# Eight-layer gated cross-attention decoder: a new order of the wide attentions' beginnings, side work and one PSUM bank

## The reference

```python
x = x + tanh(g_xattn[0]) * L0_xattn(layernorm(x), ctx, mask)      # stage 0: 8 heads of 64, masked
x = x + tanh(g_ffn[0])   * L0_ffn(layernorm(x))                   # stage 1: 16 gated attention experts
x = x + tanh(g_xattn[1]) * L1_xattn(layernorm(x), ctx)            # stage 2: 8 heads of 64
x = x + tanh(g_ffn[1])   * L1_ffn(layernorm(x))                   # stage 3: spectral
x = x + tanh(g_xattn[2]) * L2_xattn(layernorm(x), ctx)            # stage 4: 16 heads of 8
x = x + tanh(g_ffn[2])   * L2_ffn(layernorm(x))                   # stage 5: 32 experts
x = x + tanh(g_xattn[3]) * L3_xattn(layernorm(x), ctx, mask)      # stage 6: 16 heads of 64, null key, two layernorms
x = x + tanh(g_ffn[3])   * L3_ffn(layernorm(x))                   # stage 7: low rank
```

## Time and profile before

| | us |
|---|---|
| median of 3 runs (lowest, highest) | 3243.49 (3242.99, 3244.15) |
| the profiled execution's own time | 3244.79 |
| its span | 3243.0 |
| TensorE busy in it | 3020.5 (93%) |
| VectorE busy in it | 2210.6 (68%) |
| ScalarE busy in it | 1564.5 (48%) |
| GpSimd busy in it | 1207.0 (37%) |

### The profile page before, as it was taken

The page is one execution under the profiler, slowest core; times in us unless marked ns, Lnnn a source line. Parts: engine busy times, 40 slices in busy tenths (PEclk is TensorE's granted clock), DMA queues, the critical chain, the costliest instruction groups (busy, mean ns, idle before and its releaser), DMA issues. The chain is left out here.

```text
span 3243.0 us, 90979 instructions
## 1 busy us (share of the span) xinstructions
PE 3020.5 (93%) x35250; PEld 2299.3 (71%) x35250; DVE 2210.6 (68%) x6052; ACT 1564.5 (48%) x2878; POOL 1207.0 (37%) x1408
## 2 busy tenths in 40 slices
PE   6999799999997999869997999999988999999978
PEld 5888645555455888746676888888877888888864
DVE  5777656666663555667787777777767777777765
ACT  4777411111113777546663333333326666666646
POOL 5666200000003677554440000000005676676653
PEclk9999899999998999989998999999999999999999
DMA  4100165666651000011101333333320000000001
GB/s 131 40 10 7 46 173 161 184 184 178 170 160 33 12 10 10 1 51 26 26 21 54 106 106 106 106 102 102 102 72 9 11 7 10 10 10 7 10 1 53
DMA packets 110919, 212.22 MB, mean 65 GB/s; under 512 B 18752, under 2 KB 30592, under 8 KB 110240
## 3 DMA queue, kind: packets, MB, share of 16 engines
q1 hardware_dynamic: 110240, 209.19, 22.1%
q10 hardware_dynamic: 512, 0.92, 0.1%
HBM read 198.50 MB, written 5.77 MB: 63 GB/s over the span
## 5 line engine op out<-in xcount | busy, mean ns | idle before, releaser
L342 PE MATMUL ps<-parts 128*128 128x512 f32 (+2 forms) x1568 | 641.9, 409 | 45.3 <-DVE parts L975 26.5
L343 PE MATMUL ps<-parts 128*128 128x512 f32 (+2 forms) x1568 | 565.6, 361 | 0.0
L344 PE MATMUL ps<-parts 128*128 128x512 f32 (+2 forms) x1568 | 564.4, 360 | 0.0
L312 POOL TENSOR_TENSOR rstd<-mv,eps 128x4 f32<-128x4 f32 x112 | 23.7, 211 | 1225.5 <-DVE mv L295 1225.5
L342 PEld LDWEIGHTS ps<-parts 128*128 128x128 f32 (+1 forms) x1568 | 299.3, 191 | 182.9 <-ACT work L817 99.8
L1886 ACT ACTIVATE work<-ps 128x512 f32<-128x512 f32 x272 | 162.4, 597 | 454.4 <-PE ps L344 454.2
L551 POOL TENSOR_TENSOR work<-work 128x512 f32<-128x512 f32 x256 | 267.0, 1043 | 195.0 <-DVE work L945 192.9
L344 PEld LDWEIGHTS ps<-parts 128*128 128x128 f32 (+1 forms) x1568 | 298.8, 191 | 47.0
L343 PEld LDWEIGHTS ps<-parts 128*128 128x128 f32 (+1 forms) x1568 | 301.2, 192 | 13.8
L1852 PEld LDWEIGHTS ps<-early,work 128*128 128x128 f32 x2176 | 281.7, 192 | 30.1 <-DVE work L1943 11.4
L1852 PE MATMUL ps<-early,work 128*128 128x128 f32 x2176 | 289.5, 276 | 8.1 <-DVE x L2050 8.1
(11 more groups left out here) (298 smaller groups left out, 6210.5 us busy)
## 6 DMA issues: line engine op xcount, KB each, us to landing
work<-gate_rows SPq DMA_DIRECT2D x128, 512.0 KB, 5.2
work<-expert_rows SPq DMA_DIRECT2D x512, 128.0 KB, 2.9
work<-gate_rows SPq DMA_DIRECT2D x128, 256.0 KB, 7.6
work<-in_ctxT SPq DMA_DIRECT2D x72, 192.0 KB, 2.4
out<-x SPq DMA_DIRECT2D x16, 256.0 KB, 2.3
work<-work SPq DMA_DIRECT2D x224, 16.0 KB
work<-work SPq DMA_DIRECT2D x16, 128.0 KB, 3.3
early<-in_l0f_w SPq DMA_DIRECT2D x1, 1536.0 KB, 7.8
```

Source lines behind the costliest of these rows:

```text
L342: T.matmul(out, lh, rh, start=True, stop=False)
L343: T.matmul(out, lh, rl, start=False, stop=False)
L344: return T.matmul(out, ll, rh, start=False, stop=True)
```

## The change

Four things change, all in `Boot` and `wide_attention`.

1. **Values in the transposes' bank.** The value job goes to bank 4 at t=0, 2 and 3 and to bank 0 at t=1. Keys always use bank 1, queries bank 0. The waits change with it: the transposes of a step (except t=2, where it stays before attend) now wait until its values are copied out; the key job waits for the copy of the last keys; the query job waits for the copy of the last queries, and at t=1 for that of the values.
2. **Side work spread over the steps.** `take_moments` is one unit earlier, behind the shift at t=2 instead of before it at t=0; `rstd` follows at t=3 ahead of the probabilities. The spread of the low part goes from t=3 to t=1 of the next unit. In stage 6 `scale` and `take_moments` of the two layernorms and GpSimd's `finish` and `add` are placed in other steps, the addition in two halves at t=2 and t=3 of the second unit.
3. **Heads in another order.** Two key jobs, then `turn(0)`, then the other two; the second unit's keys behind the first values; the second context's split on ScalarE and DVE instead of GpSimd; the low key weights before `scale(0)`; the second unit's spreads and the biases behind the first probabilities.
4. **Gate work in the first units.** The loads of the gates, the router matrix and its gates come after x and the contexts, the first contexts in two loads; tanh and exp of the gates, the scaling of the bias rows, the norms of the router matrix are done in the units of `it` = 0, the power on GpSimd at t=2 of the second unit.

```diff
@@ Boot
-        sp.dma_start(c.ctx01[0:DC, :, :].rearrange("p a b -> p (a b)"), d["ctxT"][:, 0:2 * GT]).then_inc(self.ctx, 16)
+        sp.dma_start(c.ctx01[0:DC, 0, :], d["ctxT"][:, 0:GT]).then_inc(self.ctx, 16)
...
+        sp.dma_start(c.ctx01[0:DC, 1, :], d["ctxT"][:, GT:2 * GT]).then_inc(self.ctx1, 16)
...
@@ GpSimd, ahead of the loop
-            pool.wait_ge(low, 1)
-            split(second, c.ctx01[:, 0 if null else 1, :])
             spread(first, 0)
             split_rows(0, 0)
+            norm.rstd(pool, 1)
             spread(first, 1)
...
-            spread(second, 0), spread(second, 1)
             scale_probs(0, first, 0)
+            spread(second, 0)
@@ GpSimd, body
+                        if null:
+                            if t == 2 and u == 0 and prior:
+                                finish(it - 1)
+                            if t == 2 and u == 0 and not last:
+                                split_rows(un.g + 1, 0)
+                            if u == 1 and t in (0, 2) and not beyond:
+                                norm.rstd(pool, it + 2, t // 2)
+                        elif t == 3 and has_third(it, u, last):
+                            norm.rstd(pool, un.k + 3)
                         if not (end and t == TG - 1):
                             scale_probs(n + 1, *one_on(un, t))
...
                         if t == 0 and not last:
                             pool.wait_ge(k_done, un.k * 4 + 4)
                             split(un.next().next())
+                        if t == 1 and not end:
+                            spread(un.next(), 1)
+                        if null and prior and u == 1:
+                            if t == 2:
+                                add(it - 1)
+                            if t == 3:
+                                add_rows(it - 1)
                         if t == 3 and not last:
                             pool.wait_ge(v_full, n + 1)
-                            spread(un.next().next(), 0), spread(un.next().next(), 1)
+                            spread(un.next().next(), 0)
...
@@ TensorE, ahead of the loop
+            key_job(first, 0, 0), key_job(first, 1, 1)
...
+            turn(0)
+            for j in range(2, NJ):
+                te.wait_ge(k_done, j - 1)
                 key_job(first, j, j % 2)
-            turn(0)
-            te.wait_ge(low, 2)
-            for j in range(2):
-                te.wait_ge(k_done, j + 3)
-                key_job(second, j, j)
...
@@ TensorE, step
+    value_bank = lambda t: c.ps[:, 0 if t == 1 else 4, :]
...
                 need(te, pt_out, n)
+                if t != 2:
+                    te.wait_ge(v_done, n + 1)
...
                 te.wait_ge(pt_out, n + 1)
-                te.wait_ge(v_done, n + 1)
+                if t == 2:
+                    te.wait_ge(v_done, n + 1)
...
-                    if had_target(it, u, t, last):
-                        te.wait_ge(k_done, n + 6)
-                    value_job(*one_on(un, t), t % 2)
+                    if t == 1 and had_target(it, u, t, last):
+                        te.wait_ge(q_done, n + 6)
+                    if null and t == TG - 1 and un.p == 1:
+                        te.wait_ge(r0t_ready, un.g + 1)
+                    value_job(*one_on(un, t), value_bank(t))
...
                     if had_target(it, u, t, last):
+                        te.wait_ge(k_done, n + 6)
+                    else:
+                        te.wait_ge(q_done, NJ + 2)
+                    if t == 2:
+                        te.wait_ge(low, target.k + 1)
+                    key_job(target, j, 1)
+                    if t == 1:
+                        te.wait_ge(v_done, n + 2)
+                    elif had_target(it, u, t, last):
                         te.wait_ge(q_done, n + 6)
                     if t == 2:
-                        te.wait_ge(low, target.k + 1)
-                    key_job(target, j, 1 - t % 2)
-                    te.wait_ge(v_done, n + 2)
-                    if t == 2:
                         te.wait_ge(hq_low, target.g + 1)
-                    query_job(target, j, t % 2)
+                    query_job(target, j, 0)
@@ VectorE, ahead of the loop
+            context_low(first)
+            weights_low(0, kl, kh, wk, DC)
             norm.scale(ve, 0)
...
             weights_low(2, wvl, wvh, wv, DC)
+            context_low(second)
...
@@ VectorE, body
-                        if not null and not last and t == 0:
-                            norm.take_moments(ve, un.k + 2)
...
                             shift(n + 2, *two_on(un, t))
...
+                        if not null and t == 2 and has_third(it, u, last):
+                            norm.take_moments(ve, un.k + 3)
...
+                            if not beyond and u == 0 and t == 3:
+                                norm.take_moments(ve, it + 2)
                             if not beyond and u == 1 and t == 0:
                                 ve.wait_ge(ht_full, it + 2)
-                                norm.take_moments(ve, it + 2)
+                                norm.scale(ve, it + 2)
                             if not beyond and u == 1 and t == 1:
-                                norm.scale(ve, it + 2)
                                 norm.take_moments(ve, it + 2, 1)
-                            if not beyond and u == 1 and t == 2:
+                            if not beyond and u == 1 and t == 3:
                                 norm.scale(ve, it + 2, 1)
```

More of the change, by code:

```diff
@@ L233, in vector_first, with vector_rows @@
         V.tensor_tensor(c.w["simsq"][:, :], c.w["l0f_sim"][:, :], c.w["l0f_sim"][:, :], ALU.mult).then_inc(self.squares, 1)
+    def vector_rows(self, ve):
+        c, V = self.c, self.c.nc.vector
+        ve.wait_ge(self.rows, 16)
+        ve.wait_ge(self.tanh, 1)
+        for row, gate in ((0, 0), (1, 1), (2, 5), (3, 2), (4, 7), (5, 3)):
+            last = V.tensor_scalar(c.w["rows"][:, row, :], c.w["rows"][:, row, :], c.w["tg"][:, gate:gate + 1], None, ALU.mult)
+        last.then_inc(self.rows_ready, 1)
     def vector_second(self, ve, out):
@@ L240, in vector_second @@
         V.tensor_scalar(c.w["l0f_sig"][:, :], c.w["l0f_sig"][:, :], 1.0, None, ALU.add).then_inc(self.sig, 1)
[L241 to L245, removed]
         ve.wait_ge(self.sig, 1)
@@ L477, in banks, with has_third @@
         return ap.rearrange("p (j s) -> p s j", s=2) if len(ap.shape) == 2 else ap.rearrange("p (j s) k -> p s j k", s=2)
+    def has_third(it, u, last):
+        return not last and not (u == 1 and isinstance(it, int) and it == units // 2 - 2)
     def turns(u, t, last):
@@ L656, in value_job @@
                     lhs = [v[un.u][0:DC, t, e:e + 2, :].rearrange("c b k -> c (b k)") for v in (vh, vl)]
-                    last = product3(c, jobs[bank][:, e * NJ * DH:(e + 1) * NJ * DH], lhs, [v[0:DC, at:at + NJ * DH] for v in (wvh, wvl)])
+                    last = product3(c, out[:, e * NJ * DH:(e + 1) * NJ * DH], lhs, [v[0:DC, at:at + NJ * DH] for v in (wvh, wvl)])
                 last.then_inc(v_full, 1)
@@ L725, in _ @@
                 te.wait_ge(s0_ready, 1)
-            te.wait_ge(w_low, 3 * passes)
             te.wait_ge(q_done, NJ)
             scores(0, first, 0)
-            value_job(first, 0, 0)
+            te.wait_ge(w_low, 3 * passes)
+            value_job(first, 0, jobs[0])
             if not null:
-                te.wait_ge(ht_out, 1)
                 turn(1)
-                te.wait_ge(hq_low, 2)
-            query_job(second, 0, 1)
-            te.wait_ge(v_done, 1)
-            query_job(second, 1, 0)
-            scores(1, first, 1)
-            if boot:
-                te.wait_ge(boot.clipped, 1)
-            te.wait_ge(q_done, NJ + 2)
+            te.wait_ge(low, 2)
+            key_job(second, 0, 1)
+            te.wait_ge(v_done, 1)
+            key_job(second, 1, 0)
+            scores(1, first, 1)
+            if not null:
+                te.wait_ge(hq_low, 2)
+            for j in range(2):
+                te.wait_ge(k_done, NJ + 1 + j)
+                query_job(second, j, 1 - j)
             if not null:
                 te.wait_ge(ht_out, 2)
+            if boot:
+                te.wait_ge(boot.wo, 16)
             def body(it, last):
@@ L853, in _ @@
             weights_high(wvh, wv, DC)
-            for j in range(NJ):
-                take_key(first, j, j % 2)
+            take_key(first, 0, 0), take_key(first, 1, 1)
             take_hT(0), rows_high(0, 0)
-            for j in range(2):
-                take_key(second, j, j)
+            take_key(first, 2, 0), take_key(first, 3, 1)
+            if boot:
+                act.wait_ge(boot.ctx1, 16)
+            A.activation(ch[1][0:DC, :], c.ctx01[0:DC, 0 if null else 1, :], ACT.Copy).then_inc(high, 1)
             for j in range(NJ):
```

116 lines of the change are left out of this document (60 added, 56 removed).

## The result

The changed kernel takes 3208.11 us (median of 4 runs, 3206.64 to 3210.29) against 3243.82 (3242.99 to 3247.55) for the kernel before beside it: ratio 0.9886, 95% interval 0.9873 to 0.9899. Faster, as forecast, but by 36 us instead of 61, and 2 us above the top of the range. The profiled execution has a span of 3204.3 us, 38.7 less than before (3243.0).

The account below looks back on a forecast made before the run. TensorE (93% busy) was taken as the bound, spaced by query-job stalls and held by the softmax loop in stage 6. Savings 10.7 + 7.0 + 12 + 10.7 + 10 + 4 + 6.5 = 60.9 us gave 3183, range 3162 to 3206.

Parts of the forecast that it names:

- At t=2 ... cover 0.6 us; hidden: Stage 0: GpSimd's moved spread ends 3.0 us into t=2, probabilities at 4.1, due at 4.75, so no cost.
- nothing else is late there: Stage 0: moving the moments removes the late attend at t=1, with no other lateness; saves 7.0 us.
- the second rival: GpSimd or the ports take it back: late probabilities return stalls in half the steps, heads give two thirds; 3203 us, chance 0.25.
- stage 2, -9.3 for -10.7: Stage 2, values in the transposes' bank: 43 query-job stalls of 0.25 us go, saving 10.7 us.
- the heads, 31.8 us for 28.5: Stage starts up to the third step's transposes: savings of 12, 10 and 6.5 us in stages 0, 2 and 6.
- the rival that the loop doesn't hold: Stage 6: softmax loop not binding, so all 91 stalls and probability waits go, 27 us instead of 4; 3160 us, chance 0.14.
- The walk through stage 2's head: Stage 2's reordered start, traced hand-over by hand-over: third step at 31.5 us against 42.8; 10 us taken, bounds 7 and 13.
- the added wait for the value copy: Transposes now wait for the value copy, ending 4.1 us into a 4.71 us step: some 0.6 us to spare, no cost.
- a sign that it had named for being wrong: L759 (transposes) waiting for L551 or L817 (value copy) in stages 0 and 2.
- the collision of L311: Stage 6, norm scaling (L304 before) beside GpSimd's split: cost 0 to 0.5 us per eight steps, 0.5 taken.
- 17.7: Stage 0, third to last step: saving of 17.7 us, from 10.7 for stalls and 7.0 for the late attend.
- the gate work: First units of stage 0: power on GpSimd ahead of probabilities and small products inside one loop cost about 1.5 us.

Follow-up runs that it names:

- e1: Changed kernel with VectorE's mask rows of the next unit in stage 0 moved from ahead of the t=2 shift to behind the t=1 shift; 3187.86 us.
- e2: Changed kernel with the second half of GpSimd's spread back at t=3 in stage 0 alone, mask rows still at t=2; 3187.9 us.
- e5: Changed kernel with GpSimd's spread at t=2 of stage 0 first waiting for VectorE's mask rows, order unchanged; 3192.84 us.
- e10: Changed kernel with an unused VectorE mask-row scaling added at t=2 ahead of the shift in each unit of stage 2; 3214.68 us.
- e11: Changed kernel with an unused VectorE maximum over the same mask added at t=2 ahead of the shift in each unit of stage 2; 3208.12 us.
- e3_bank_alone: Kernel before with only the values' bank changed, and the waits that belong to it; 3240.08 us, ratio 0.9981 to the kernel before.
- e7_bank_undone: Kernel of e1 with the values' banks and waits put back as in the kernel before; 3207.76 us, ratio 0.9869 to the kernel before.
- e6_split_later: Kernel of e1 with, in stage 6's second units, GpSimd's L539 moved behind t=1's probabilities and mask rows to t=0 ahead of the sums; 3184.99 us.
- e4_rstd_behind: Changed kernel with the norm's reciprocal deviation behind, instead of ahead of, the probabilities at t=3 in stage 0; 3205.85 us.
- e8_best: Kernel of e6_split_later with GpSimd's power of the similarity norms in the last instead of first pair of units of stage 0; 3185.73 us.

## Why the prediction was right and wrong

*The step that failed* is "At t=2 ... cover 0.6 us; hidden", with "nothing else is late there" of the paragraph on stage 0. I timed GpSimd's instructions at t=2 and asked when the probabilities would be due, and they were on time (they end 3.93 us into the step; 4.1 was forecast). I did not ask what VectorE does at t=2 beside them: the mask rows, 0.29 us in the row of before, which began before GpSimd's next instruction there. The spread that I moved made it 2.56 us, and t=3 6.27 instead of 4.72. I knew the effect, priced it at L304 in stage 6 and in the heads, and never looked through the other VectorE scalings for one that the moved spread would meet. e1, e2 and e5 show the cause, each by another hand: 20 us in the time, 19.6 us from third to last step of stage 0 (321.7 against 302.1). The nearest was the second rival (GpSimd or the ports take it back, 0.25, 3203), but it priced late probabilities, returned stalls and collisions in the heads, not a VectorE instruction held at t=2 and a wait of 1.5 us at attend; that its 3203 lies near 3208 is luck.

The Trainium skill, SBUF — State Buffer, Who interferes with whom, says that tensor_scalar can enter a 2-port mode and then excludes GpSimd, while tensor_reduce on this chip never contends. The twins of e10 and e11 agree: 2575 and 368 ns. The same section of the Trainium skill says that whoever issues first has the ports for a whole instruction. The row agrees for L539 and L311, but L949 stayed blocked over three GpSimd instructions in a row; counting only the instruction that it met (L552, to 171.75) would have priced it at 1 us. Nor did it wait for the whole gapless run: in the steady steps it got in ahead of the fourth, L326, which would have made it 3.7 us or more, while one instance of the first pass lasted 3.76 us, over L326 too. What decides this isn't known.

*Held in size:* the stall of 0.25 us and 4.72 us for ordinary steps; stage 2, -9.3 for -10.7; the heads, 31.8 us for 28.5; and eight steps of stage 6, forecast near 43.2, which took 42.95 (the rival that the loop doesn't hold wanted less than 42.3). The walk through stage 2's head said 31.5 us and the head took 31.7, better than I trusted it. No run separated the heads' new order from the rest; that they gained shows in the stretches alone.

*Two smaller misses inside these.* The last seven steps of stage 2 became 2 us longer, 28.6 to 30.7. The bank edit does that: 30.5 in e3_bank_alone, 28.6 in e7_bank_undone. Where no key and query jobs are left, nothing covers the added wait for the value copy, a cost that the prediction put at nothing; L777 waits for L846 there, 3.1 us in 4 waits, a sign that it had named for being wrong. In stage 6 the step with the collision of L311 became half a microsecond longer, as forecast (5.82 to 6.28), but the collision explains only half of that: without it e6_split_later has 6.04, and with it but without the bank edit e7_bank_undone has 6.01.

*Stage 0 without the collision* still gives 12 us from third to last step, not 17.7, though eight steps fall by 2.63 us, as much as forecast. Most of the rest is in the gate work, a term mis-sized. From the third step to the end of the sixteenth e1_mask_earlier takes 73.1 us (38.58 to 111.72), no less than before (72.6, 54.58 to 127.17), where 14 ordinary steps would be 69:

```profile
38.58 0.60 PE L777 MATMUL ps<-ident,work 128*128 128x128 f32 x4
...
111.72 0.49 PE L777 MATMUL ps<-ident,work 128*128 128x128 f32 x3
```

I had counted 1.5 us for the six row products, the power and the small products inside the loop; the stretch is 4.3 us longer than its ordinary steps, 1 us of it the stall told at the end, so they cost about 3, some of it again row products held beside the spread (six L244 took 2.77 us).

*Stage 2's sum was right as a sum only.* I gave 10.7 us of stage 2 to the bank; e3 shows that it is worth nothing there (305.3 us from third to last step, 305.5 before) until the side work is moved, since the chain of deviation and scaling is next; with it moved it is worth 8.0. The prediction named the bound of each step without jobs, but not that of t=1.

## What to carry to other kernels

When an instruction of GpSimd is moved, list every VectorE scaling, copy and two-operand product that it will now run beside, however short, and price each between the one GpSimd instruction that it meets and the whole run that follows without a gap: here it was three instructions of four. Reductions of such data can be left out (e11). Look for the next bound in each step of the period, not in the ordinary one alone: an edit that frees six steps of eight can be returned in the other two, and then it is worth something only together with the edit that frees those.

## What the runs showed of the hardware

A VectorE instruction of 0.24 us can last 2.58 us beside three GpSimd instructions, with no work of its own being more; and the reduction over the same data, beside the same three, isn't lengthened (368 ns, 367 with none of the spread beside it).

In some profiles TensorE stands still once in the first pass of the loop in stage 0, in the midst of 32 like matmuls and waiting for nothing that the profile shows: 0.5 us in e1_mask_earlier, 2.9 in e2_spread_back, 1.4 in e5_spread_waits, 2.3 in e6_split_later; not at all in the kernel before, the changed kernel, e4_rstd_behind and e7_bank_undone. In e8_best:

```profile
72.67 0.38 PE L703 MATMUL ps<-work 64*64 64x64 f32 x9
75.40 0.52 PE L703 MATMUL ps<-work 64*64 64x64 f32 x20 [2.35 <-issue]
```

After it the granted clock falls for some microseconds to its lower level of 1.2 GHz (windows: start:end, us, busy time of five engines, clock, DMA share, GB/s):

```profile
71.00:75.00 4.00, 2.05 (x23) 1.74 (x22) 1.98 (x4) 1.95 (x4) 3.15 (x4) 1.00 1.10 265
76.00:80.40 4.40, 4.40 (x43) 3.63 (x34) 3.10 (x7) 2.21 (x4) 0.65 (x1) 0.53 0.69 135
80.40:82.50 2.10, 2.10 (x11) 2.07 (x10) 0.89 (x2) 1.08 (x3) 0.97 (x1) 0.50 0.02 5
```

The same pair of steps took 11.1 us in e1_mask_earlier, 14.8 in e2_spread_back, 14.2 in e6_split_later, 15.8 here and 10.4 in the changed kernel's profile, where 10.1 are ordinary. That is up to 6 us in one execution, more than the last three kernels differ by. With one profile for each kernel it isn't shown whether it changes from execution to execution or with the kernel. The DMA engines are full in that stretch (share 1.10, 265 GB/s) and quiet behind it, but they are as full in the changed kernel (1.09, 280 GB/s from 70 to 74 us), which doesn't stall, so this alone is not the cause. In the five profiles named with a stall TensorE goes on 1.3 to 1.5 us after a 16 KB packet has landed on q8, the queue of instructions (here 73.89 and 75.40 us). A sequencer that waits for its next instructions would fit; no run tried it.
